# A GRU-fed expert layer: the stretch ahead of the recurrence in another order and in larger pieces

## The chip, the cores and the metric

One core of a Trainium2 chip runs the whole program. The metric is device microseconds (us) of one execution. Five engines take part: TensorE (PE), VectorE (DVE), ScalarE (ACT), GpSimd (POOL) and SyncE (SP); the last issues most of the transfers. Each engine runs its own list of instructions in order, and they meet through semaphores only.

## The reference

A GRU runs over 256 time steps for 8 sequences of width 512, and its states feed an expert layer with 8 experts (two per token) and a shared expert. What the change touches lies ahead of the first time step.

```python
def cell(h, x):                        # 256 times, one after the other
    gi = x @ W_ih + b_ih               # x: (8, 256, 512), W_ih: (512, 1536)
    gh = h @ W_hh + b_hh               # W_hh: (512, 1536)
    i_r, i_z, i_n = jnp.split(gi, 3, axis=-1)
    h_r, h_z, h_n = jnp.split(gh, 3, axis=-1)
    r = jax.nn.sigmoid(i_r + h_r)
    z = jax.nn.sigmoid(i_z + h_z)
    n = jnp.tanh(i_n + r * h_n)
    return (1.0 - z) * n + z * h
...
logits = h @ w_gate                    # softmax, the two best of 8 experts
gu = jnp.einsum('th,ehf->etf', h, w_gate_up); act = silu(g) * u
routed = combine of jnp.einsum('eti,eih->eth', act, w_down)
return x + routed + silu_and_mul(h @ w_sh_gate_up) @ w_sh_down
```

## The kernel before, in words

Every float32 matrix is kept as two float16 halves, a high and a low one, and a product of two matrices takes three float16 products (`PROD`). To split a matrix it must be scaled by a power of two, and that needs a bound of its largest magnitude first. So each matrix goes through the same steps: its transfer lands; it is scanned (VectorE takes a row maximum with `rowmax`, ScalarE a row sum of magnitudes with `accum_out`, each over a part of it); the bounds of several matrices are spread over all 128 partitions by two tiny TensorE products, `spread_cross` and `spread_back`, with VectorE's `spread_rows` and `spread_scale` between and behind them; `floors` makes scales of them and releases `scaled`; then `high` on ScalarE writes the high half of a piece and `low` on VectorE the low half.

There are three such rounds ahead of or early in the recurrence. Round 1 holds x's first block (`PX0`) and W_ih (`PIH`). Round 2 holds W_hh, the router's weights, h0 and x's block 1 (`PHH` and the three behind it). Round 3 holds the rest of x (`PX`).

A weight matrix of 512 x 1536 lies in 12 slots of 128 x 512. The raw float32 numbers lie `SHIFT = 2` slots behind the place of their halves, so a high half may be written only when the low half of two slots before has been read (the wait on `ih_lo` or `hh_lo` in `high_ih` and `high_hh`).

`gates(n, c)` on TensorE multiplies W_ih with a block of 32 time steps of x: n // 12 is the block, n % 12 the slice of 128 output columns, and c the quarter of the inner width. The 12 products of block 0 come ahead of the recurrence, with six PSUM banks; the first six fill them, and n = 6 and on wait until `gates_out` (ScalarE for even n, VectorE for odd n) has emptied the bank. Later blocks are spread over the time steps by `make_plan`, a list scheduler: for each piece of work it has an engine, a cost in us, what it comes after, an earliest step and a due step. From it come the orders of all engines within the loop over t.

A time step is `recur(t)` on TensorE (32 small products into psG), then `step(t)` on VectorE, which begins with two transposes out of psG and ends with the new state, and three tanh on ScalarE between. Behind `step(t)` every engine does its planned work of that step, and ScalarE then `keep(t)`. `place(t)` puts the input gates of step t beside psG's numbers; VectorE's second transpose waits for it.

Right ahead of step 0, VectorE's list ends with `x_low(1)`, the low half of x's block 1, and ScalarE's with `x_high(1)` and three sums of x's rest, `sum_x(3)` to `sum_x(5)`; `sum_x(0)` to `sum_x(2)` stand behind the sum over W_hh.

## Time and profile before

| what | value |
|---|---|
| three runs, median (lowest to highest) | 1200.42 us (1195.88 to 1204.8) |
| profiled execution, its own time | 1195.19 us |
| span of its trace | 1193.4 us |
| busy: PE, DVE, ACT, POOL | 87%, 71%, 48%, 17% |
| first transpose of step 0, of the last step | 51.33 us, 1033.57 us |

The span runs from the first to the last record of the trace; 1.8 us of the execution lie outside it. A share of busy time is a mean over the whole program: up to 51.33 us no time step has begun, up to about 1037 us the 256 steps run, and the rest is the tail of the expert layer.

### The profile page before, as it was taken

Reading aid. Unit: us, or ns where it says so; the run is one execution under the profiler, and the core shown is the slowest. Engines: PE = TensorE matmul, PEld = TensorE weight load, DVE = VectorE, ACT = ScalarE, POOL = GpSimd, SP = SyncE. Lnnn points to the kernel's source line nnn. Section 1 sums busy time; section 2 is a strip of 40 time slices with the busy share of each in tenths; the row PEclk is TensorE's granted clock in tenths of the full one; section 3 lists DMA queues with packets and bytes.
Section 4 is the critical chain, followed back from the end, with each engine's and each line's share of the span. In section 5 each row is a group of like instructions: output and inputs, shape, how many; then the busy total and the mean of one; then the engine's idle time right before and its main releaser. Section 6 shows DMA issues by size and latency. Waiting matters only on the chain.

```text
span 1193.4 us, 35909 instructions
## 1 busy us (share of the span) xinstructions
PE 1036.9 (87%) x13452; PEld 623.1 (52%) x13452; DVE 850.0 (71%) x4089; ACT 573.3 (48%) x1877; POOL 206.2 (17%) x213
## 2 busy tenths in 40 slices
PE   2789888889999898999899989998998898889894
PEld 2556555556665454555455545554555454555452
DVE  5898999868889888677867787678787778721111
ACT  4755555655555543445344434443444444435442
POOL 0200011020110212111211121112120112233332
PEclk9999999999999999999999999999999999999897
DMA  8943455381864753623451234234342144488694
GB/s 307 402 147 97 144 180 186 107 205 56 294 237 173 197 193 73 230 75 61 125 178 29 55 101 166 56 55 174 129 126 55 28 143 134 121 296 278 181 288 56
DMA packets 68829, 183.13 MB, mean 153 GB/s; under 512 B 7737, under 2 KB 40288, under 8 KB 61344
## 3 DMA queue, kind: packets, MB, share of 16 engines
q1 hardware_dynamic: 45632, 107.74, 25.5%
q0 software_dynamic: 23024, 73.11, 23.1%
q8 instruction: 106, 1.74, 0.6%
q14 instruction: 67, 0.55, 0.2%
HBM read 137.01 MB, written 52.87 MB: 159 GB/s over the span
## 4 chain that ended last, share of the span: by engine, by line
PE 51%; DVE 27%; ACT 10%; issue 7%; DMA 3%; POOL 0%; POOLq 0%; SPq 0%; ACTq 0%; DVEq 0%
PE psG L715 17%; PE psG L721 14%; PE psU L778 6%; DVE arena L1046 5%; DVE arena L1044 5%; ACT arena L1429 4%; ACT arena L1425 4%; PE psS L824 3%; DVE arena L1054 3%; DVE arena L1069 3%; DVE arena L1065 3%; DVE arena L1056 3%; PE psD L790 3%; DVE arena L1048 2%; PE psO L845 2%
## 5 line engine op out<-in xcount | busy, mean ns | idle before, releaser
L715 PE MATMUL psG<-arena 128*32 128x384 f16 x4096 | 213.8, 329 | 76.1 <-DVE arena L1069 68.2
L1425 ACT ACTIVATE arena<-arena 128x32 f32<-128x32 f32 x256 | 58.6, 229 | 336.7 <-DVE arena L1048 335.3
L721 PE MATMUL psG<-arena 128*32 128x384 f16 x4096 | 211.9, 327 | 3.7 <-issue 3.7
L778 PE MATMUL psU<-arena 128*128 128x256 f16 (+1 forms) x1920 | 203.7, 253 | 0.2 <-DVE arena L940 0.2
L1044 DVE STREAM_TRANSPOSE arena<-psG 128x128 f32<-128x128 f32 x256 | 81.1, 317 | 144.8 <-PE psG L721 138.2
L778 PEld LDWEIGHTS psU<-arena 128*128 128x128 f16 x1920 | 157.7, 99 | 49.1 <-issue 13.6
L715 PEld LDWEIGHTS psG<-arena 128*32 128x32 f16 x4096 | 86.2, 96 | 175.0 <-DVE arena L1069 141.9
L1625 POOL DMA_INDIRECT y<-arena x55 | 87.6, 1593 | 393.4 <-DVE arena L1046 312.2
L721 PEld LDWEIGHTS psG<-arena 128*32 128x32 f16 x4096 | 109.9, 97 | 60.9 <-issue 4.4
L1046 DVE STREAM_TRANSPOSE arena<-psG 128x256 f32<-128x256 f32 x256 | 104.1, 407 | 0.0
L790 PE MATMUL psD<-arena 128*128 128x512 f16 x384 | 97.6, 382 | 4.9 <-DVE arena L1264 4.9
L824 PE MATMUL psS<-arena 128*128 128x512 f16 x372 | 92.3, 380 | 1.7 <-ACT arena L1497 1.5
L1441 ACT ACTIVATE arena<-arena 128x64 f16<-128x64 f16 x256 | 63.9, 250 | 37.1 <-DVE arena L1074 36.1
L1429 ACT ACTIVATE arena<-arena 128x32 f32<-128x32 f32 x256 | 58.7, 229 | 39.4 <-DVE arena L1056 16.3
L940 DVE SCALAR_TENSOR_TENSOR arena<-arena 128x1024 f16<-128x1024 f32 (+1 forms) x68 | 73.4, 1091 | 2.7 <-ACT arena L1334 2.3
L1427 ACT ACTIVATE arena<-arena 128x32 f32<-128x32 f32 x256 | 58.7, 229 | 26.8
L1334 ACT ACTIVATE arena<-arena 128x1024 f16<-128x1024 f32 (+1 forms) x68 | 66.4, 986 | 8.3 <-DVE arena L940 4.2
L700 PE MATMUL psS<-arena 128*128 128x256 f16 x528 | 67.0, 273 | 1.0 <-issue 0.7
L700 PE MATMUL psO<-arena 128*128 128x256 f16 x528 | 67.4, 276 | 0.0
L1065 DVE TENSOR_TENSOR arena<-arena 128x32 f32<-128x32 f32 x256 | 49.2, 192 | 22.4 <-ACT arena L1429 0.7
L1051 DVE TENSOR_REDUCE arena<-arena 128x32 f32<-128x96 f32 x256 | 64.0, 250 | 0.0
L1050 DVE TENSOR_REDUCE arena<-arena 128x32 f32<-128x96 f32 x256 | 63.1, 246 | 0.0
(166 smaller groups left out, 1557.7 us busy)
## 6 DMA issues: line engine op xcount, KB each, us to landing
arena<-expert_weights SPq DMA_DIRECT2D x39, 1536.0 KB, 8.6
arena<-wgu POOLq DMA_DIRECT2D x32, 512.0 KB, 5.5
expert_weights<-arena POOLq DMA_DIRECT2D x9, 1536.0 KB, 6.8
gi_scratch<-arena SPq DMA_DIRECT2D x84, 128.0 KB, 2.0
arena<-gi_scratch SPq DMA_DIRECT2D x14, 768.0 KB, 5.6
arena<-wd POOLq DMA_DIRECT2D x16, 512.0 KB, 5.7
arena<-x SPq DMA_DIRECT2D x8, 512.0 KB, 4.0
hidden_rows<-arena SPq DMA_DIRECT2D x16, 256.0 KB
```

The lines of the kernel that those rows point to most:

```text
L700: r = e.matmul(ps, half(W_IH + fc // 4 * 4 + c, pw)[:, (fc % 4) * 128:(fc % 4) * 128 + 128], x_half(b, c // 2, px)[:, (c % 2) * 256:(c % 2 ...
L715: e.matmul(psG[32 * j:32 * j + 32, 0:384], prev[:, c, 2:6].rearrange("p q n -> p (q n)"), whv[c][1][:, :, :, 32 * j:32 * j + 32], start=(c ...
L721: r = e.matmul(psG[32 * j:32 * j + 32, 0:384], prev[:, c, 0:4].rearrange("p q n -> p (q n)"), whv[c][0][:, :, :, 32 * j:32 * j + 32], star ...
L778: r = e.matmul(psU[u % 2][:, 256 * gu:256 * gu + width], half(W_GS + ex * 4 + c, pw)[:, o:o + 128], hh[:, 1 - ph, c, first:first + width], ...
L790: r = e.matmul(ps[:, 0:512], AH[u % 3][:, pa, tc * 128:tc * 128 + 128], half(W_DS + n, pw), start=(n == 0 and j == 0), stop=(n == 7 and j ...
L824: r = e.matmul(up_bank(k)[:, 0:512], hT[k % 2][:, ph, c], ew_half(k, c, pw), start=(c == 0 and j == 0), stop=(c == KC - 1 and j == 2))
L1044: e.transpose(Tt[:, 0:4, 0:32], psG[:, 0:128].rearrange("p (f m) -> p f m", m=32)).then_inc(tr_r, 1)
L1046: e.transpose(Tt[:, 4:12, 0:32], psG[:, 128:384].rearrange("p (f m) -> p f m", m=32)).then_inc(tr_zn, 1)
L1065: e.tensor_tensor(zc, zc, qq, ALU.mult).then_inc(g_m, 1)
L1425: e.activation(Ur, Ur, ACT.Tanh, scale=reg_tr).then_inc(th_r, 1)
L1429: e.activation(qq, qq, ACT.Tanh, scale=reg_tn).then_inc(th_n, 1)
L1625: e.indirect_dma_start(y, by(index), out, None, compute_op=ALU.add).then_inc(added, 16)
```

## The change: what it does

- The transfers of W_ih and W_hh are cut: four of 768 KB for W_ih, and 768, 768, 768, 256 and 512 KB for W_hh, each with a semaphore of its own. x's block 1 has its own place (`x_src(1)`, slots 8 and 9 of ring 0) and is issued before the small loads and without a wait; before, it came behind them and waited until `x_low(0)` had been done. The raw weights lie four slots behind their halves (`WSHIFT = 4`), the last two slots of W_hh's raw numbers in ring 1.
- W_ih is scanned in quarters as they land; the last quarter is shared by VectorE and ScalarE (768 columns each).
- W_hh's bound is taken earlier: ScalarE sums slots 0 to 2 ahead of `x_high(0)`, and slots 3 to 5 and 10, 11 behind the first third of W_ih; VectorE takes slots 6 to 9 there. x's block 1 is bounded by ScalarE (`x1_sum`) instead of VectorE.
- Round 2's `spread_cross` stands behind gates n = 1 and `spread_back` behind n = 2; before, both stood behind n = 3.
- `high_ih`, `high_hh`, `low_ih` and `low_hh` take two slots (128x1024) at a time: 6 instructions for each matrix and engine where there were 12.
- Of block 0's `gates_out`, ScalarE takes 8 and VectorE 4 (before 6 and 6).
- `recur(0)` waits for W_hh's low halves by quarters of the inner width, not for all at once.
- `x_low(1)` moves behind step 0. The six `sum_x` move behind steps 0 to 3 (2, 2, 1, 1). Round 3 moves from steps 1 to 4 to steps 4 to 7. In the plan, gates of block 1 begin at step 1, `scan_load` and `d_sum` at step 3, x's block 2 at step 8. The plan has 363 steps as before; from step 42 on, every step holds the same work as before.

The instructions of TensorE from the first product of gates to the second time step, before (psU, psD, psS and psO are the banks of gates, psT that of the bounds, psG that of the recurrence):

```order
3 L700 MATMUL psU<-arena 128x256 x24
4 L700 MATMUL psD<-arena 128x256 x24
5 L676 MATMUL psT<-arena 4x128
6 L680 MATMUL psT<-arena 128x4
7 L700 MATMUL psS<-arena 128x256 x12
8 L700 MATMUL psO<-arena 128x256 x12
9 L700 MATMUL psU<-arena 128x256 x24
10 L700 MATMUL psD<-arena 128x256 x24
11 L700 MATMUL psS<-arena 128x256 x12
12 L700 MATMUL psO<-arena 128x256 x12
13 L715 MATMUL psG<-arena 32x384 x16
```

And the same stretch of TensorE in the changed kernel:

```order
3 L709 MATMUL psU<-arena 128x256 x24
4 L685 MATMUL psT<-arena 4x128
5 L709 MATMUL psD<-arena 128x256 x12
6 L689 MATMUL psT<-arena 128x4
7 L709 MATMUL psD<-arena 128x256 x12
8 L709 MATMUL psS<-arena 128x256 x12
9 L709 MATMUL psO<-arena 128x256 x12
10 L709 MATMUL psU<-arena 128x256 x24
11 L709 MATMUL psD<-arena 128x256 x24
12 L709 MATMUL psS<-arena 128x256 x12
13 L709 MATMUL psO<-arena 128x256 x12
14 L725 MATMUL psG<-arena 32x384 x16
```

The first bounding product of round 2 (psT, 4x128) moved ahead by 24 matmuls and the second by 12; the rest stands as it did.

ScalarE from the split of W_ih to step 0, before (128x2x512 is x, 128x512 a slot of a weight matrix; 128x1024 x3 are the sums over x's rest, 128x2x128 the emptying of a bank, 128x8x8 `place`):

```order
4 L1334 ACTIVATE arena<-arena 128x512 x8
5 L1391 ACTIVATE arena<-arena 128x4608
6 L1369 ACTIVATE arena<-arena 128x1024 x3
7 L1334 ACTIVATE arena<-arena 128x512 x4
8 L1360 ACTIVATE arena<-psU,arena 128x2x128
...
20 L1411 ACTIVATE arena<-arena 128x8x8
21 L1334 ACTIVATE arena<-arena 128x2x512
22 L1369 ACTIVATE arena<-arena 128x1024 x3
23 L1420 TENSOR_LOAD arena
24 L1421 TENSOR_LOAD arena
25 L1425 ACTIVATE arena<-arena 128x32
```

ScalarE in the changed kernel, from the sums of W_ih to the end of step 0:

```order
4 L1361 ACTIVATE arena<-arena 128x1536
5 L1348 ACTIVATE arena<-arena 128x2x512 x3
6 L1361 ACTIVATE arena<-arena 128x1536
7 L1361 ACTIVATE arena<-arena 128x1024
8 L1417 ACTIVATE arena<-arena 128x1024
9 L1348 ACTIVATE arena<-arena 128x2x512 x5
...
25 L1443 TENSOR_LOAD arena
26 L1444 TENSOR_LOAD arena
27 L1448 ACTIVATE arena<-arena 128x32
28 L1450 ACTIVATE arena<-arena 128x32
29 L1452 ACTIVATE arena<-arena 128x32
30 L1436 ACTIVATE arena<-arena 128x8x8
31 L1389 ACTIVATE arena<-arena 128x1024 x2
```

The sum over nine slots of W_hh became sums of three, three and two, and the sums over x's rest left the stretch ahead of the tanh of step 0 (L1425, now L1448); two of them stand behind it.

The diff, cut to its core:

```diff
+WSHIFT = 4
...
-            p.add("PE", ("gates", n, c), 0.37, before, due=due)
+            p.add("PE", ("gates", n, c), 0.37, before, step=1, due=due)
...
+        def ih_raw(k, n):
+            return raw(W_IH + WSHIFT + k, n)
+
+        def hh_raw(k, n):
+            return ring(1, 6 + k - 10, n) if k >= 10 else raw(W_HH + WSHIFT + k, n)
+
+        def x_src(b):
+            return ring(0, 8, 2) if b == 1 else view(xp_raw, 1024, F32)
...
-            for q in range(2):
-                piece(wih, raw(W_IH + SHIFT + 6 * q, 6), 6 * q, 6, ld_ih[q])
-            for q in range(2):
-                piece(whh, raw(W_HH + SHIFT + 6 * q, 6), 6 * q, 6, ld_hh[q])
+            for q in range(4):
+                piece(wih, ih_raw(3 * q, 3), 3 * q, 3, ld_ih[q])
+            for q, (k, n) in enumerate(((0, 3), (3, 3), (6, 3), (9, 1), (10, 2))):
+                piece(whh, hh_raw(k, n), k, n, ld_hh[q])
+            load(x_src(1), x[:, 1024:2048], ld_x1)
...
-            e.wait_ge(x_lo, 1)
-            load(view(xp_raw, 1024, F32), x[:, 1024:2048], ld_xp)
+            e.wait_ge(hh_sum, 3)
             piece(x, ring(0, 0, 6), 4, 6, ld_xrest[0])
-            e.wait_ge(hh_sum, 1)
             piece(x, ring(1, 0, 6), 10, 6, ld_xrest[1])
...
                 for c in range(KC):
+                    if t == 0:
+                        e.wait_ge(hh_lo, (2, 3, 5, 6)[c])
...
-            for n in range(4):
-                for c in range(KC):
-                    gates(n, c)
-            spread_cross(2, PHH, 4)
-            spread_back(2, 4)
-            for n in range(4, 12):
+            for n in range(12):
+                if n == 2:
+                    spread_cross(2, PHH, 4)
+                if n == 3:
+                    spread_back(2, 4)
                 for c in range(KC):
                     gates(n, c)
...
             def low_hh(k):
-                low(raw(W_HH + SHIFT + k, 1), half(W_HH + k, 0), half(W_HH + k, 1), col(SHH), hh_hi, k + 1, hh_lo)
+                at = CH * (W_HH + 2 * k)
+                low(pair(hh_raw(2 * k, 2)), halves(at, 0), halves(at, 1), col(SHH), hh_hi, k + 1, hh_lo)
...
             x_low(0)
-            for k in range(8):
+            for k in range(2):
                 low_ih(k)
+            for q in (2, 3):
+                e.wait_ge(ld_hh[q], 16)
+            link(rowmax(mx[:, 38:39], hh_raw(6, 4)))
             e.wait_ge(ld_small, 128)
...
+            e.wait_ge(hh_sum, 3)
+            e.wait_ge(x1_sum, 1)
+            rowmax(gcol[:, PHH:PHH + 1], mx[:, 36:40]).then_inc(spread_cols, 1)
+            low_ih(2)
             spread_rows(2, 4)
+            low_ih(3)
...
-            for k in range(12):
-                if k % 2:
-                    gates_out(k)
+            for k, ready in enumerate(((), (1, 4), (), (7,), (), (10,))):
+                for n in ready:
+                    gates_out(n)
                 low_hh(k)
...
-            x_low(1)
...
             e.wait_ge(ld_ih[1], 16)
+            sum_weights(ih_raw(3, 3), ring(1, 0, 3), 42, ih_sum)
+            e.wait_ge(ld_ih[3], 16)
+            sum_weights(ih_raw(9, 3)[:, 768:1536], ring(1, 3, 3)[:, 0:768], 45, ih_sum)
+            e.wait_ge(ld_hh[0], 16)
+            sum_weights(hh_raw(0, 3), ring(0, 0, 3), 36, hh_sum)
             e.wait_ge(scaled, 1)
             x_high(0)
-            for k in range(8):
+            for k in range(2):
                 high_ih(k)
+            e.wait_ge(ld_hh[1], 16)
+            sum_weights(hh_raw(3, 3), ring(0, 3, 3), 37, hh_sum)
+            e.wait_ge(ld_hh[4], 16)
+            sum_weights(hh_raw(10, 2), view(hb0 + 4096, 1024, F32), 39, hh_sum)
+            e.wait_ge(ld_x1, 16)
+            e.activation(view(hb0 + 8192, 1024, F32), x_src(1), ACT.Abs, accum_out=gcol[:, PX1:PX1 + 1]).then_inc(x1_sum, 1)
+            for k in range(2, 6):
                 high_ih(k)
...
-            for k in range(3, 6):
-                sum_x(k)
...
+                for k in ((0, 1), (2, 3), (4,), (5,))[t] if t < 4 else ():
+                    sum_x(k)
```

## Rows read from the trace of the kernel before

**Rows 1.** The page: shares of the span in the chain that ended last.

```profile
PE 51%; DVE 27%; ACT 10%; issue 7%; DMA 3%; POOL 0%; POOLq 0%; SPq 0%; ACTq 0%; DVEq 0%
```

**Rows 2.** Timeline of VectorE, first transpose of steps 0, 1, 8, 53, 255.

```profile
51.33 0.31 DVE L1044 STREAM_TRANSPOSE arena<-psG 128x128 f32<-128x128 f32 x1
...
55.95 0.32 DVE L1044 STREAM_TRANSPOSE arena<-psG 128x128 f32<-128x128 f32 x1 [1.26 <-PE psG L721]
...
83.23 0.32 DVE L1044 STREAM_TRANSPOSE arena<-psG 128x128 f32<-128x128 f32 x1
...
261.05 0.32 DVE L1044 STREAM_TRANSPOSE arena<-psG 128x128 f32<-128x128 f32 x1 [5.22 <-PE psG L721]
...
1033.57 0.32 DVE L1044 STREAM_TRANSPOSE arena<-psG 128x128 f32<-128x128 f32 x1 [1.01 <-PE psG L721]
```

**Rows 3.** Timeline of VectorE up to step 0 (start, length, instruction, idle before).

```profile
12.85 1.94 DVE L915 TENSOR_REDUCE arena<-arena 128x1 f32<-128x1536 f32 x2 [0.35 <-DMA arena<-wih]
...
18.41 2.61 DVE L940 SCALAR_TENSOR_TENSOR arena<-arena 128x1024 f16<-128x1024 f32 x3 [1.22 <-ACT arena L1334]
...
29.16 1.41 DVE L915 TENSOR_REDUCE arena<-arena 128x1 f32<-128x2 f32 x2 [1.43 <-ACT arena L1391]
...
34.70 1.41 DVE L940 SCALAR_TENSOR_TENSOR arena<-arena 128x512 f16<-128x512 f32 x2
...
49.15 0.15 DVE L936 SCALAR_TENSOR_TENSOR arena<-arena 128x1 f32<-128x1 f32 x1
...
50.13 1.28 DVE L940 SCALAR_TENSOR_TENSOR arena<-arena 128x1024 f16<-128x1024 f32 x1
```

**Rows 4.** Timeline of ScalarE up to the first tanh of step 0.

```profile
12.85 1.48 ACT L1383 ACTIVATE arena<-arena 128x1536 f32<-128x1536 f32 x1 [10.82 <-DMA arena<-wih]
...
24.94 4.03 ACT L1391 ACTIVATE arena<-arena 128x4608 f32<-128x4608 f32 x1
...
28.97 1.04 ACT L1369 ACTIVATE arena<-arena 128x1024 f32<-128x1024 f32 x1
...
48.83 1.13 ACT L1334 ACTIVATE arena<-arena 128x1024 f16<-128x1024 f32 x1
...
52.99 0.21 ACT L1425 ACTIVATE arena<-arena 128x32 f32<-128x32 f32 x1
```

**Rows 5.** Timeline of TensorE: gates, round 2's two products, the first recur.

```profile
22.68 5.10 PE L700 MATMUL psU<-arena 128*128 128x256 f16 x24 [6.29 <-DVE arena L940]
27.62 2.78 PE L700 MATMUL psD<-arena 128*128 128x256 f16 x24
30.63 0.38 PE L676 MATMUL psT<-arena 128*4 128x128 f32 x2 [0.23 <-DVE arena L915]
31.38 0.38 PE L680 MATMUL psT<-arena 4*128 4x4 f32 x2 [0.37 <-DVE arena L928]
...
49.28 0.84 PE L715 MATMUL psG<-arena 128*32 128x384 f16 x16 [2.08 <-DVE arena L940]
```

**Rows 6.** Windows of 1 us, TensorE: busy (instructions), granted clock, DMA share, GB/s.

```profile
24.00:25.00 1.00, 1.00 (x6) 1.00 1.04 442
...
39.00:40.00 1.00, 1.00 (x7) 0.50 0.84 356
```

**Rows 7.** Transfers issued from 2.5 to 3.2 us: KB each, us to landing.

```profile
arena<-wih SPq DMA_DIRECT2D x1, 1536.0 KB, 10.7
arena<-whh SPq DMA_DIRECT2D x1, 1536.0 KB, 13.9
```

**Rows 8.** Transfers issued from 20.0 to 20.3 us, the same columns.

```profile
arena<-x SPq DMA_DIRECT2D x1, 1536.0 KB, 7.0
arena<-x SPq DMA_DIRECT2D x1, 512.0 KB, 3.7
```

**Rows 9.** Timeline of SyncE's queue: issue of the last small load.

```profile
11.30 3.16 SPq L578 DMA_DIRECT2D arena<-bhh  x1
```

**Rows 10.** Transfers issued from 11 to 12 us: KB each, us to landing.

```profile
arena<-bhh SPq DMA_DIRECT2D x1, 6.0 KB, 10.5
```

128 lines of the change are left out of this document (62 added, 66 removed).

## The prediction

> **What bounds the kernel now.** I read the chain of waits first. It is half TensorE and a quarter VectorE [rows 1], so no engine alone is the bound: what sets the end is a serial chain. The list of VectorE's first transposes shows which. From step 53 to step 255 they are 772.52 us apart for 202 steps, 3.82 us each [rows 2], and what is planned beside the steps fits into them with little over. The changed plan holds the same work in every step from 42 on, so behind that step a saving neither grows nor shrinks: the whole tail comes as much earlier as step 42 does. The question is thus where step 0 begins (51.33 us), how long it takes (4.62 us, against 3.8) and what steps 1 to 41 add.
>
> Next I read the three engines ahead of step 0. The reader is to see that nobody is idle for long, but that the work comes in a row. VectorE has W_ih's bound at 14.79 us, two microseconds behind the landing [rows 3]; TensorE starts the gates at 22.68 us and comes to round 2 of the bounds at 30.63 us, which VectorE's columns released at 30.57 us [rows 3, 5], and these waited for ScalarE's 4.03 us sum over W_hh, begun only at 24.94 us [rows 4], although W_hh's first half had landed at 2.62 + 13.9 = 16.5 us [rows 7]. From 34.70 to 49.15 us VectorE takes lows and banks without a pause worth the name [rows 3]: this stretch of 14.45 us is bound by VectorE. Then come small instructions and `x_low(1)`, and step 0. In step 0 VectorE had its numbers early, but ScalarE's first tanh began at 52.99 us, behind three sums over x's rest [rows 4].
>
> **The change part by part**, in the trace's own time.
>
> *W_ih's bound.* Its last transfer lands at 12.8 us as before, if pieces stream. Behind it stood a row maximum over 1536 columns and a tiny one, 1.94 us together [rows 3]; the last quarter is now shared, 768 columns each: half of 1.77, and 0.17, is 1.05 us on VectorE. On ScalarE the 768 columns are 0.75 to 0.95 us by half of 1.48 [rows 4] and something fixed: level. **-0.9 us**; the columns stand at 13.9.
>
> *To the gates.* From the columns to `x_low(0)` it took 14.79 to 18.41, 3.6 us, and this stays, if the new sum over slots 0 to 2, ahead of `x_high(0)`, is through by then. It begins when the first W_hh piece lands, halfway between 12.8 and 16.5, at 14.7, and takes 1.6: 16.3, against the release of `scaled` at about 16.4. It just fits; if it lands later, each 0.1 us costs 0.1. Then x and two W_ih pieces of 1024 columns: 1.28 and twice 1.19 (x3 of mixed size took 2.61, and pieces overlap by 0.09) is 3.7, where five pieces took 4.2. The gates start at 17.5 + 3.8 = 21.3. **-1.4 us** in all.
>
> *Round 2.* ScalarE ends the second W_ih piece at 19.7 and then has sums over 1536, 1024 and 1024 columns (1.48, 1.04, 1.04 and 0.1 between [rows 4]): 23.4. VectorE's 2048 columns are 2.3 us from 21.3 on. So the columns stand at 23.8 instead of 30.57. But TensorE is then within gates 0 and 1, ahead of round 2 in its list. Their 24 matmuls took 5.10 us, the next 24 took 2.78 [rows 5], and at 24 us six matmuls passed in 1 us, about as at 39 us, where the granted clock is recorded as 0.50, that is 1.2 GHz [rows 6]; the 1.00 recorded at 24 us I do not believe. Again TensorE comes out of about 5 idle microseconds (before, 6.29 [rows 5]), so I take the slow 5.1: `spread_cross` at 26.3, **-4.3 us**. If the clock rises sooner, 3.9 instead of 5.1 gives 25.1; if all of gates 2 is slow too, 1.2 later. `spread_back` stood 0.75 behind `spread_cross`; now twelve matmuls stand between, 1.4 at the fast rate, and VectorE's `low_ih(3)`, 1.28, runs under them: 28.0 against 31.38, **-3.4 us**. From there to VectorE's first free moment it took 34.70 - 31.38 = 3.3 and does so again: 31.3.
>
> *Lows and banks.* Before, 16 slots and 6 banks in 14.45 us [rows 3]. A pair of slots was 1.41 alone, 1.6 with ScalarE's turn; a piece of 1024 is 1.28 [rows 3], and overlapping 1.19. Now 8 pieces and 4 banks (0.45 each, what is left of 14.45 when 16 slots at 0.66 and 1.2 of waits are taken off, over 6): 9.5 + 1.8 = 11.3, and 0.1 of waiting. ScalarE's turn of 1.13 a piece [rows 4] plus 8 banks at 0.45 stays under it. VectorE is through at 42.7 against 49.15, **-6.4 us** in all. TensorE keeps up: gates 7 waits for VectorE's bank 1 until about 35.3, then five products at 1.35 end at 42.1. The last quarter of W_hh's low halves is what `recur(0)` waits for: its products end at 43.7, when VectorE is through with its small instructions (1.0 us, 49.15 to 50.13). `x_low(1)`, 1.2 us ahead of the transposes, is gone. Step 0 starts at 43.8 instead of 51.33: **-7.5 us**.
>
> *Step 0.* No sums stand ahead of the tanh, so it should take the ordinary 3.81: **-0.8 us**, and -8.3 us at step 1. The cover of what moved: `x_low(1)`, 1.28, lies in VectorE's idle end of step 0 (matmuls of `recur(1)`), and TensorE needs it just behind; two sums, 2.2 us, lie in what ScalarE has free in a step, which I put at 2.7 us: 3.81 less four short instructions of some 0.21 [rows 4] and the waits between them.
>
> *Steps 1 to 41.* Before, steps 1 to 7 took 27.28 us [rows 2], 0.6 over seven plain ones, for round 3; the same VectorE work is there, only later. New is that step 1 holds two sums, a bank and `keep` (2.9 us in the 2.7) and step 3 two sums and a bank (2.9), and that TensorE has 21 gate matmuls in steps 1 and 3: **+0.3 us**. The transfers they trigger (`scan_load` at x_sum 3 and 6, steps 1 and 3) have until step 9.
>
> Sum: -7.5 - 0.8 + 0.3 = **-8.0 us**. The profiled execution of 1195.19 would become 1187.2. It lay 5.2 us below the median of the runs; I subtract from the median: 1200.42 - 8.0 = **1192.4 us**.
>
> Bounds: step 0 at 43.3 (fast clock early) to 45.0 (gates 2 slow, a late landing), and +0 to +2 in steps 1 to 41: a gain of 4.5 to 8.5 us, so 1191.9 to 1195.9, and beside it the spread of medians; three runs lay 9 us apart.
>
> **The rivals.**
>
> *Pieces pay for themselves.* W_ih landed at 12.8 and W_hh's first half at 16.5, 3.7 us for 1.5 MB, while a load of 512 KB that found the queue empty took 3.7 from issue to landing and the 1536 KB behind it landed 3.7 later [rows 7, 8]. For: nothing shows pieces under 1.5 MB one behind the other. Against: that 512 KB did not delay its follower. If each additional piece cost 1.9 (3.7 less the 1.8 of its bytes at the streaming rate is the fixed part), W_ih's bound would come 3.8 us later and the end with it: 1196.2. The Trainium skill, "DMA: Bandwidth & Descriptors", section "Measured (HBM→SBUF, 128 partitions, SWDGE, issued from GpSimd)", asks for transfers of at least 1 MiB to reach 75% of peak, and speaks against the cut; at three quarters of the rate it too would put W_ih some 3 us later. Pieces of a full queue are not what rows 8 show delayed, so 7 in 100.
>
> *The small loads come last (slower).* They now stand behind x's block 1 and seven further pieces, and round 2 needs all eight (`ld_small`). The last was held 3.16 us at its issue and landed at 11.30 + 10.5 = 21.8 [rows 9, 10]. My estimate is 22.8: 1.2 later for the 512 KB ahead of them. They decide from about 25 us on, and each microsecond beyond costs one. If the hold is paid by each of the eight, because the queue is full of pieces by then, 8 x 3.16 from about 9.9 is 35, landing at about 37: step 0 at 55.6, 4.3 later than before, and the end at 1200.42 + 4.3 - 0.8 + 0.3 = 1204.2. [...] 6 in 100.
>
> *Given back in the first steps.* ScalarE's sums overrun, gates come late behind `x_low(1)`, and stores of gates compete with W_gu and W_d, whose loads go out at the same pace as before but meet earlier steps. Each slip of a tanh lengthens a step. Seven steps at +0.4 give back 3 us: 1195.4. 15 in 100.
>
> *The single stall.* Step 53 begins 261.05, 5.22 us after VectorE fell idle, waiting for TensorE [rows 2], which waited for nothing shown, in the middle of a recur. It costs some 4.7 us. The changed list has the same matmuls up to there, so I leave it where it is. The Trainium skill, "Runtime: NRT & Kernel Launch", section "Instruction fetch mechanics", says that instructions come in blocks by a queue of their own and that this is mostly hidden; if this was a fetch under the loads of that moment, it can vanish or come twice. Gone: 1187.7, 6 in 100; a second one: 1197.1, 6 in 100.
>
> **How the numbers follow.** Forecast 60 in 100, its own range 1188.5 to 1197.5. The likeliest is 1192.4; I give 1192.5. The range for 8 in 10 takes in the spread of the runs and the rivals but the slower one: 1186.5 to 1199.5. A measurement of this kernel can tell about 1% (12 us) from no change. Faster by over 1% needs 1188.4 or less: the vanished stall and the low side of the forecast, 0.17. Slower by over 1% needs more than the worst rival, 0.03. Within 1%: 0.80.
>
> **What would show it.** Right: gates at about 21.3 us, `spread_cross` of round 2 released by TensorE itself at 26, not by VectorE; step 0's first transpose at 43.3 to 45; step 1 3.8 us later; step 8 about 8 us earlier than before; steps from 42 on unchanged. Wrong: a first piece of W_ih or a small load that VectorE waits for beyond 25 us; a slow clock in gates 7 to 11 (1.2 us for each twelve matmuls); steps 1 to 20 above 3.9 us; a new stall of TensorE under the scan loads.

## The result, and the profile after

The changed kernel takes 1191.28 us (median) against 1203.3 us for the kernel before on the same chip, a ratio of 0.9905 (95% interval 0.9881 to 0.9929), -11.4 us. Two later repeats on two chips gave 0.9934 (0.9909 to 0.9959) and 0.9925 (0.9902 to 0.9947), -8.0 and -9.0 us. The mean of the three ratios is 0.9921, or -9.5 us. The forecast was -8.0 us and 1192.5. That 1191.28 lies so close to 1192.5 is in part luck: the forecast started from 1200.42, the median of three runs of the kernel before, which over eight runs is 1203.3. As a gain, -11.4 is more than the 4.5 to 8.5 us that the prediction gave for it; the repeats of -8.0 and -9.0 lie in it and just beyond it.

The timeline of VectorE in the kernel after, in the same columns as [rows 2] and [rows 3]: the last scans of W_ih, the pieces of W_hh, then the first transposes of steps 0, 1, 8, 42, 50, 53, 54 and 255.

```profile
11.14 3.08 DVE L924 TENSOR_REDUCE arena<-arena 128x1 f32<-128x1536 f32 x3 [2.00 <-DMA arena<-wih]
17.83 3.68 DVE L949 SCALAR_TENSOR_TENSOR arena<-arena 128x1024 f16<-128x1024 f32 x3 [1.22 <-ACT arena L1348]
21.43 2.66 DVE L924 TENSOR_REDUCE arena<-arena 128x1 f32<-128x2048 f32 x4
...
30.87 3.67 DVE L949 SCALAR_TENSOR_TENSOR arena<-arena 128x1024 f16<-128x1024 f32 x3
...
41.25 1.27 DVE L949 SCALAR_TENSOR_TENSOR arena<-arena 128x1024 f16<-128x1024 f32 x1
...
43.63 0.32 DVE L1056 STREAM_TRANSPOSE arena<-psG 128x128 f32<-128x128 f32 x1
...
47.43 0.32 DVE L1056 STREAM_TRANSPOSE arena<-psG 128x128 f32<-128x128 f32 x1
...
74.70 0.31 DVE L1056 STREAM_TRANSPOSE arena<-psG 128x128 f32<-128x128 f32 x1
...
204.88 0.32 DVE L1056 STREAM_TRANSPOSE arena<-psG 128x128 f32<-128x128 f32 x1
...
237.75 0.32 DVE L1056 STREAM_TRANSPOSE arena<-psG 128x128 f32<-128x128 f32 x1 [2.23 <-remote]
...
251.12 0.32 DVE L1056 STREAM_TRANSPOSE arena<-psG 128x128 f32<-128x128 f32 x1 [2.45 <-PE psG L731]
254.92 0.32 DVE L1056 STREAM_TRANSPOSE arena<-psG 128x128 f32<-128x128 f32 x1
...
1027.75 0.32 DVE L1056 STREAM_TRANSPOSE arena<-psG 128x128 f32<-128x128 f32 x1 [1.01 <-PE psG L731]
```

The columns of W_ih stand at 14.22 us, and VectorE is through with the pieces at 42.52 (before 49.15 [rows 3]). Step 0 starts at 43.63 us against 51.33 [rows 2], step 1 at 47.43 against 55.95, step 8 at 74.70 against 83.23. From step 53 (251.12) to step 255 it is 776.6 us here, 772.5 before: no part of the gain comes from there.

TensorE in the kernel after, its first products up to recur(0), answers to [rows 5]:

```profile
21.57 4.33 PE L709 MATMUL psU<-arena 128*128 128x256 f16 x24 [5.75 <-DVE arena L949]
25.83 0.38 PE L685 MATMUL psT<-arena 128*4 128x128 f32 x2
26.14 1.48 PE L709 MATMUL psD<-arena 128*128 128x256 f16 x12
27.55 0.38 PE L689 MATMUL psT<-arena 4*128 4x4 f32 x2
...
35.14 1.47 PE L709 MATMUL psU<-arena 128*128 128x256 f16 x12 [1.86 <-DVE arena L967]
...
41.78 1.15 PE L725 MATMUL psG<-arena 128*32 128x384 f16 x16
42.75 0.82 PE L731 MATMUL psG<-arena 128*32 128x384 f16 x16
```

The row at 25.83 has no bracket: round 2's product waits for nobody, only for the 24 slow matmuls ahead of it. VectorE's columns had been there since 21.43 + 2.66 = 24.09 us.

ScalarE in the kernel after, against [rows 4]: the sum over the first W_hh piece in the gap ahead of `x_high(0)`, and the first tanh, which VectorE alone releases now.

```profile
14.89 1.48 ACT L1361 ACTIVATE arena<-arena 128x1536 f32<-128x1536 f32 x1 [0.94 <-DMA arena<-whh]
...
16.65 3.23 ACT L1348 ACTIVATE arena<-arena 128x1024 f16<-128x1024 f32 x3 [0.18 <-DVE arena L933]
...
44.45 0.23 ACT L1448 ACTIVATE arena<-arena 128x32 f32<-128x32 f32 x1 [0.67 <-DVE arena L1060]
```

### The profile page after: what moved, and what is told of

Read it like the earlier page. It is cut to its first block, busy times and chain, and to the rows that moved or that the text cites. A ratio compares the mean times of both kernels' runs of the same rounds, so it can differ in the third digit from the quotient of the medians.

```text
span 1187.0 us, 35881 instructions
## 1 busy us (share of the span) xinstructions
PE 1033.3 (87%) x13452; PEld 621.2 (52%) x13452; DVE 846.4 (71%) x4075; ACT 574.1 (48%) x1875; POOL 206.3 (17%) x213
## 3 DMA queue, kind: packets, MB, share of 16 engines
q8 instruction: 106, 1.74, 0.6%
## 4 chain that ended last, share of the span: by engine, by line
PE 51%; DVE 26%; ACT 8%; issue 8%; DMA 4%; POOL 1%; another core or an unknown queue 0%; POOLq 0%; SPq 0%; DVEq 0%; ACTq 0%
PE psG L725 17%; PE psG L731 14%; PE psU L788 5%; DVE arena L1058 5%; DVE arena L1056 5%; ACT arena L1448 3%; ACT arena L1452 3%; DVE arena L1066 3%; DVE arena L1081 3%; DVE arena L1068 3%; PE psD L800 3%; PE psS L834 3%; DVE arena L1077 3%; DVE arena L1060 2%; PE psO L855 2%
## 5 line engine op out<-in xcount | busy, mean ns | idle before, releaser
L725 PE MATMUL psG<-arena 128*32 128x384 f16 x4096 | 214.0, 329 | 77.8 <-DVE arena L1081 68.4
L1448 ACT ACTIVATE arena<-arena 128x32 f32<-128x32 f32 x256 | 58.7, 229 | 333.3 <-DVE arena L1060 333.3
L731 PE MATMUL psG<-arena 128*32 128x384 f16 x4096 | 211.8, 326 | 1.6 <-issue 1.6
L788 PE MATMUL psU<-arena 128*128 128x256 f16 (+1 forms) x1920 | 203.5, 253 | 0.2 <-DVE arena L949 0.2
L788 PEld LDWEIGHTS psU<-arena 128*128 128x128 f16 x1920 | 157.5, 98 | 48.7 <-issue 12.9
L725 PEld LDWEIGHTS psG<-arena 128*32 128x32 f16 x4096 | 86.3, 96 | 176.9 <-DVE arena L1081 140.5
L731 PEld LDWEIGHTS psG<-arena 128*32 128x32 f16 x4096 | 110.0, 97 | 59.1 <-issue 2.5
L949 DVE SCALAR_TENSOR_TENSOR arena<-arena 128x1024 f16<-128x1024 f32 x56 | 71.2, 1278 | 1.7 <-ACT arena L1348 1.6
L709 PE MATMUL psS<-arena 128*128 128x256 f16 x528 | 67.4, 273 | 0.5 <-ACT arena L1384 0.3
L709 PE MATMUL psO<-arena 128*128 128x256 f16 x528 | 66.1, 273 | 0.4 <-ACT arena L1384 0.4
L1348 ACT ACTIVATE arena<-arena 128x1024 f16<-128x1024 f32 x56 | 63.3, 1136 | 4.4 <-DVE arena L949 3.2
## 6 DMA issues: line engine op xcount, KB each, us to landing
arena<-gi_scratch SPq DMA_DIRECT2D x14, 768.0 KB, 5.5
```

Of the source, the lines that this page charges most:

```text
L709: r = e.matmul(ps, half(W_IH + fc // 4 * 4 + c, pw)[:, (fc % 4) * 128:(fc % 4) * 128 + 128], x_half(b, c // 2, px)[:, (c % 2) * 256:(c % 2 ...
L725: e.matmul(psG[32 * j:32 * j + 32, 0:384], prev[:, c, 2:6].rearrange("p q n -> p (q n)"), whv[c][1][:, :, :, 32 * j:32 * j + 32], start=(c ...
L731: r = e.matmul(psG[32 * j:32 * j + 32, 0:384], prev[:, c, 0:4].rearrange("p q n -> p (q n)"), whv[c][0][:, :, :, 32 * j:32 * j + 32], star ...
L788: r = e.matmul(psU[u % 2][:, 256 * gu:256 * gu + width], half(W_GS + ex * 4 + c, pw)[:, o:o + 128], hh[:, 1 - ph, c, first:first + width], ...
L1448: e.activation(Ur, Ur, ACT.Tanh, scale=reg_tr).then_inc(th_r, 1)
```

## The experiments

There were twelve runs, in three groups of four; the runs of a group share a chip and the executions of the kernel before, whose medians were 1206.02, 1201.16 and 1195.77 us. Differences in microseconds are a ratio times that median; the plain difference of two medians is up to 1.6 us off from it. "Changed kernel" is the kernel after. The changed kernel was run in the first and third groups, and there no 95% interval of a variant lies clear of its own; so the medians alone tell little and the traces carry the argument.

### Both kernels again

*The kernel before, unchanged.* 

> The kernel before, unchanged, for a second trace of it. Theory A (the gain is the stretch up to step 1, the rest is scatter): the first transpose again at 51.3 us and step 1 at 55.9 us, within 0.3; the ratio to the runs of before 1.000 within 0.003; what differs from the first trace (span 1193.4 us) is how long single steps between 8 and 255 are held up. Theory B (the stall of TensorE at step 53 is a property of the kernel before): the step before 53 is again above 6 us. Rival C (the stall is chance): a plain 3.8 us there and stalls elsewhere.

Measured: 0.9993 (0.9972 to 1.0014), so the comparison tells some 0.2% from nothing. Step 0 came at 52.14 us, 0.8 later than expected, and step 1 at 56.04, as expected. The step before 53 again took over 6 us (7.65), so theory B holds and rival C falls.

*The changed kernel, unchanged.* 

> The changed kernel, unchanged, for a second trace. Theory A: step 0 at 43.6 us, step 1 at 47.4 us, step 8 at 74.7 us, each within 0.3, and a ratio to before of 0.993 (8.0 us, the sum of the prediction), if the scatter of single steps is the same in both. Rival D (the change also lessens the stalls behind step 42): a ratio of 0.990 again, and fewer or shorter held-up steps than in the traces of before.

Measured: 0.9934 (0.9909 to 0.9959), -8.0 us, as expected. The trace missed: step 0 came at 44.00 us, step 1 at 49.08 and step 8 at 76.40, 0.4, 1.7 and 1.7 later than expected. *And once more, in the third group.* 

> The changed kernel once more, so that the other kernels of this call have it on their own chip: between 8 and 11.4 us under the kernel before, the two differences seen so far. Step 0 at 43.6 to 44.0 us in its trace; a hold of 1.7 to 2.2 us at step 49 and of 1.9 to 5 us at steps 52 and 53.

Measured: 0.9925 (0.9902 to 0.9947), -9.0 us. Its step 0 came at 44.68 us, 0.7 later than expected; the hold at step 49 did not come, and that at steps 52 and 53 took 8.60 and 5.67 us, 6.6 us in excess. Five traces of the two kernels give the start of steps in a table:

```
trace          step 0   step 1   step 42   step 48   step 54
before          51.33    55.95    214.16    237.01    265.58
before again    52.14    56.04    214.25    237.11    264.24
after           43.63    47.43    204.88    227.74    254.92
after again     44.00    49.08    206.58    229.44    259.75
after, third    44.68    49.62    207.41    230.26    260.07
```

At step 42 the changed kernel is ahead by 9.3, 7.6 and 6.8 us, 7.9 in the mean. From 42 to 48 all five take 22.85 or 22.86 us. From 48 to 54 they take 28.57, 27.13, 27.18, 30.31 and 29.81, where the six steps alone would take 22.9. So what the change is known to do is done at step 42. From step 54 to step 255 the two traces of the kernel before take 768.0 and 773.6 us, the three of the changed kernel 772.8, 775.7 and 768.4; five traces can't tell whether anything of the gain is given back there.

### Larger pieces

```diff
-                at = CH * (W_IH + 2 * k)
-                low(pair(ih_raw(2 * k, 2)), halves(at, 0), halves(at, 1), col(SIH), ih_hi, k + 1, ih_lo)
+                for s in (2 * k, 2 * k + 1):
+                    low(ih_raw(s, 1), half(W_IH + s, 0), half(W_IH + s, 1), col(SIH), ih_hi, s + 1, ih_lo)
```

and so for W_hh, for ScalarE's high halves and for the waits on them.

> The changed kernel with the low halves of both weights computed again in 16 pieces of 512 columns instead of 8 of 1024; scans, landings, round 2 and the order of the sums stay as changed. If the larger pieces are worth what the sum of the prediction took (14.45 us of pieces before against 11.4), step 0 starts 2 to 3 us later than the changed kernel's 43.6 to 44.0 us and the median is 2 to 3 us higher. If the pieces pay for themselves (VectorE was already waiting for ScalarE's high halves and not for its own work), step 0 moves by less than 0.5 us and so does the median.

Measured: 0.9947 (0.993 to 0.9963), -6.4 us. The changed kernel itself has no run in this group; its three runs elsewhere had -8.0 to -11.4, and the next kernel, in this group, -10.0. VectorE's timeline of the same stretch, and one row of TensorE:

```profile
31.28 4.06 DVE L949 SCALAR_TENSOR_TENSOR arena<-arena 128x512 f16<-128x512 f32 x6
...
41.53 1.42 DVE L949 SCALAR_TENSOR_TENSOR arena<-arena 128x512 f16<-128x512 f32 x2 [0.85 <-ACT arena L1348]
...
43.40 1.41 DVE L949 SCALAR_TENSOR_TENSOR arena<-arena 128x512 f16<-128x512 f32 x2
```

```profile
35.94 2.72 PE L709 MATMUL psU<-arena 128*128 128x256 f16 x12 [2.25 <-DVE arena L967]
```

Six pieces of 512 take 4.06 us where three of 1024 take 3.67. From the first piece to the last VectorE needs 13.53 us, against 11.65 in the changed kernel, and step 0 starts at 45.91, 1.2 to 2.3 us later than in its three traces. Of the 1.9 us between the two, 0.85 is a wait for ScalarE's high half: TensorE's twelve matmuls took 2.72 us here, against 1.47, so ScalarE had to wait 2.00 us for the bank psD ahead of that half. TensorE had stood idle for 2.25 us ahead of them, against 1.86; whether the smaller pieces brought this about or chance did, one trace can't tell, and the profiled execution, 1205.61 us, lay 10 us above the median of its kernel. What is left, 1.0 us, is VectorE's own pieces, as the prediction had it (16 slots at 0.66 against 8 pieces at 1.19). So the theory holds for about half of the 1.9 us; step 0 comes 2 us later than in the two faster traces with both halves of it.

### Round 2 of the bounds, later and sooner

```diff
-                if n == 2:
-                    spread_cross(2, PHH, 4)
-                if n == 3:
-                    spread_back(2, 4)
+                if n == 4:
+                    spread_cross(2, PHH, 4)
+                    spread_back(2, 4)
```

> The changed kernel with both products of round 2 behind gates 3 again. Theory A (TensorE's list sets round 2): spread_cross 2.6 us later (28.5 instead of 25.8), and since low_ih(3) then stands between VectorE's maximum and its scales, 2.2 to 2.5 us later at the first transpose (46.0). Rival (the lows bind VectorE anyway, so round 2 may come later): under 1 us.

Measured: 0.9942 (0.9921 to 0.9963), -7.0 us, 1.0 us slower than the changed kernel beside it; the intervals overlap. The trace is clearer: TensorE's round 2 and the wait that comes of it,

```profile
21.60 4.93 PE L709 MATMUL psU<-arena 128*128 128x256 f16 x24 [5.75 <-DVE arena L948]
...
29.08 0.38 PE L685 MATMUL psT<-arena 128*4 128x128 f32 x2
...
38.12 1.47 PE L709 MATMUL psU<-arena 128*128 128x256 f16 x12 [2.80 <-DVE arena L966]
```

and step 0 at 46.61 us, 2.6 later than the changed kernel of that group. Theory A holds in the trace, with both times 0.6 us later than worked out.

The other way, `spread_cross` ahead of gates 1 (n == 1) and `spread_back` ahead of gates 2, with VectorE's `spread_rows` ahead of `low_ih(2)` and `low_ih(3)` behind `floors`:

> The changed kernel with round 2 of the spread sent by TensorE before it starts on the gates of the second quarter, not after, and with VectorE's part of it ahead of the low half of the third quarter. Theory: TensorE reaches round 2 at 25.8 us with nothing to wait for, since its own slow matmuls stand in front of it; put ahead of them it goes at about 24.1, the scale is known 1.7 us sooner, and about 1 us of that reaches step 0, so the median is 1 us lower. Rival: the low halves on VectorE set the end alone, and whatever round 2 gains is given back in a wait for the next low half: step 0 within 0.3 us, the median unchanged.

Measured: 0.9917 (0.9898 to 0.9937), -10.0 us. TensorE:

```profile
21.75 2.74 PE L709 MATMUL psU<-arena 128*128 128x256 f16 x12 [5.75 <-DVE arena L949]
24.43 0.42 PE L685 MATMUL psT<-arena 128*4 128x128 f32 x2
```

Round 2 goes at 24.43 us, 1.4 sooner than in the kernel after, but step 0 starts at 43.34, 0.3 sooner: 18.91 us behind `spread_cross(2)`, where it is 17.80 in the kernel after. So 1.1 us is given back on VectorE, which now has `low_ih(3)` and the setting up one behind the other, instead of a piece of 1.26 us under TensorE's products. Against the kernel after the rival holds; against the other two traces of the changed kernel (44.00 and 44.68) step 0 is 0.7 and 1.3 sooner, as the theory had it. The medians can't tell 1 us.

### W_ih's scans by pairs of quarters

```diff
-            e.wait_ge(ld_ih[0], 16)
+            for q in range(2):
+                e.wait_ge(ld_ih[q], 16)
             link(rowmax(mx[:, 41:42], ih_raw(0, 3)))
-            e.wait_ge(ld_ih[2], 16)
+            for q in (2, 3):
+                e.wait_ge(ld_ih[q], 16)
```

and the same two waits ahead of ScalarE's sums.

> The changed kernel with W_ih's scans waiting for its quarters in pairs: scans 0 and 1 start when quarter 1 has landed, the rest when quarter 3 has; each scan stays the same size and on the same engine. Theory: what the quarters buy is the scan of quarter 2 beside the landing of quarter 3. Without it VectorE scans 1.75 and 0.95 us after the last landing at about 13.0, so the columns are ready at 15.8 and not 14.2, and with nothing to catch up on behind them step 0 and the median are 1.2 to 1.6 us later. Rival: later on VectorE waits 1.2 us for ScalarE's high half and ScalarE waits for W_hh, so half of it is caught up: 0.5 us.

Measured: 0.995 (0.9919 to 0.9982), -6.0 us, 3.0 us slower than the changed kernel beside it; the intervals overlap. TensorE:

```profile
23.24 4.45 PE L709 MATMUL psU<-arena 128*128 128x256 f16 x24 [5.76 <-DVE arena L949]
27.62 0.38 PE L685 MATMUL psT<-arena 128*4 128x128 f32 x2
```

The gates start 1.44 us later than in the changed kernel's trace of this group (21.80), step 0 only 0.74 later (45.42 against 44.68). Not by VectorE's catching up, as the rival had it: the same 24 matmuls took 4.45 us here and 5.15 there, so round 2 went 0.75 later (27.62 against 26.87), and step 0 followed it to the hundredth. In the three traces of the changed kernel and in this one step 0 comes 17.80, 17.80, 17.81 and 17.80 us behind `spread_cross(2)`. That product, held by TensorE's slow start, sets the stretch.

### The sums of x back ahead of step 0

```diff
             place(0)
             x_high(1)
+            for k in range(3):
+                sum_x(k)
```

with one more in each of steps 0 to 2, as before, and `x_low(1)` back ahead of step 0.

> The changed kernel with one part undone: x_low(1) and three of the sums over x's rest stand ahead of step 0 again. Theory A: VectorE has 1.2 us more ahead of the first transpose (44.9 instead of 43.6), and ScalarE's first tanh comes at 46.9 behind x_high(1) (42.7 to 43.8) and three sums (3.2), 1.1 later than the transposes ask: step 1 at 49.8 instead of 47.4, the whole 2.4 us slower than the changed kernel. Rival (the steps behind absorb it, since there they have fewer sums): less than 1 us slower.

Measured: 0.9955 (0.9933 to 0.9977), -5.4 us, 2.5 us slower than the changed kernel beside it (by the medians 1.0); the intervals overlap. ScalarE's third sum and its first tanh in this kernel:

```profile
45.77 1.04 ACT L1388 ACTIVATE arena<-arena 128x1024 f32<-128x1024 f32 x1
46.81 0.21 ACT L1449 ACTIVATE arena<-arena 128x32 f32<-128x32 f32 x1
```

The tanh comes 1.8 us behind the transposes of 45.02 and step 0 takes 6.02 us. The changed kernel has its tanh 0.82 us behind them, so the sums cost 1.0 us of step 0. Step 0 starts 1.0 later than in the changed kernel's trace of this group (`x_low(1)`), step 1 2.0, step 8 2.4, step 42 2.3. The price came out as expected, 2.4 us, in the trace and in the ratio. Step 1 itself came at 51.04 us, not 49.8, because `recur(1)` is slow here as well:

```profile
48.24 1.47 PE L725 MATMUL psG<-arena 128*32 128x384 f16 x16 [4.65 <-DVE arena L1082]
```

### The slow matmuls, and the holds at steps 49 and 52

Two things differ from trace to trace of one kernel. The first is TensorE's rate. In the second trace of the changed kernel `recur(1)` is slow. Its TensorE:

```profile
46.27 1.47 PE L725 MATMUL psG<-arena 128*32 128x384 f16 x16 [2.32 <-DVE arena L1081]
47.53 1.50 PE L731 MATMUL psG<-arena 128*32 128x384 f16 x16
```

and its window from 44 to 48 us (busy time and instructions of TensorE, of its weight loads, VectorE, ScalarE and GpSimd, then the granted clock, DMA share and GB/s):

```profile
44.00:48.00 4.00, 1.73 (x24) 0.92 (x28) 3.55 (x14) 3.07 (x10) 0.00 (x0) 0.75 0.52 217
```

The same stretch of the kernel after, at full clock:

```profile
44.00:48.00 4.00, 2.02 (x37) 1.27 (x38) 3.74 (x15) 3.06 (x9) 0.00 (x0) 1.00 0.55 229
```

Step 0 takes 5.08 us in the one and 3.80 in the other. The fast one is the exception. In all twelve traces of the changed kernel and its variants TensorE stands idle for 2.32 us or more ahead of `recur(1)`, and in ten of them it or the matmuls right behind it are slow: steps 0 and 1 together take 7.76 us in the kernel after and in one other, and 8.93 to 9.25 in nine more, 1.2 to 1.5 us longer (`sums_back`, with the sums on top, 10.45). Neither trace of the kernel before has this, for between `recur(0)` and `recur(1)` stood gates of block 1:

```profile
51.52 1.47 PE L700 MATMUL psS<-arena 128*128 128x256 f16 x12 [0.75 <-issue]
52.83 0.82 PE L700 MATMUL psO<-arena 128*128 128x256 f16 x6
```

The change moved them to step 1, since they need `x_low(1)`. What ScalarE's sums covered is something else and smaller: in the second trace of the kernel before `recur(0)` was slow, behind 3.19 idle microseconds, and step 0 came 0.8 us later, yet step 1 at 56.04 against 55.95, as the sums ended last either way. The sums do not cover a slow `recur(1)`, as their return shows: it took 1.47 us there too. No run keeps gates in step 0 of the changed kernel, so what that would give, 1.2 to 1.5 us by these traces less what the gates cost there, is an estimate.

The second is a hold of TensorE in `recur(53)`. The kernel before, TensorE:

```profile
255.53 0.33 PE L721 MATMUL psG<-arena 128*32 128x384 f16 x3
259.55 1.46 PE L721 MATMUL psG<-arena 128*32 128x384 f16 x13 [3.69 <-issue]
```

The kernel after:

```profile
248.35 0.33 PE L731 MATMUL psG<-arena 128*32 128x384 f16 x3
250.25 0.82 PE L731 MATMUL psG<-arena 128*32 128x384 f16 x13 [1.56 <-issue]
```

All twelve traces without added matmuls break that group of 16 at the same place, three and thirteen, for 0.90 to 4.06 us. In the five microseconds before TensorE went on there is one packet of the instruction queue q8, in each of the fourteen traces. The DMA view of such a window (packets, MB, share of 16 engines) in the kernel after, from 246.0 us:

```profile
q8 instruction: 1, 0.02, 38.4%
```

in the second run of it, from 250.0 us:

```profile
q8 instruction: 1, 0.02, 25.9%
```

and in the next kernel, from 248.0 us:

```profile
q8 instruction: 1, 0.02, 14.7%
```

Share times 16 engines times the window's 0.5 us is how long the packet took: 3.1, 2.1 and 1.2 us. The page of the kernel after has 106 of them at 0.6% of 16 engines' span, 1.1 us each, for 26904 matmuls and weight loads of TensorE, 254 a packet; the kernels with 40 more matmuls have 107. So q8 is very likely TensorE's. In windows of 0.1 us the packets start at 246.1, 250.3 and 248.2 us, so they ended at about 249.2, 252.4 and 249.4, and TensorE went on 1.0 to 1.3 us behind that. This speaks for a hold that ends when the packet is in. But in the third of them the packet had ended ahead of the hold (249.74 us), so its transfer alone does not fill the hold. Two kernels test this. The first moves the DRAM-to-DRAM copies that GpSimd issues at 235 us (y<-xt, hidden_rows<-hpad, with an expert's load right behind) to other steps, by the planner's numbers alone:

```diff
-        p.add("POOL", ("hid_init", b), ..., step=8 + 11 * b, due=8 + 11 * b)
-        p.add("POOL", ("y_init", b), ..., step=20 + 10 * b, due=20 + 10 * b)
+        hs = (8, 13, 25, 32, 41, 63, 74, 85)[b]
+        ys = (14, 25, 31, 40, 60, 70, 80, 90)[b]
+        p.add("POOL", ("hid_init", b), ..., step=hs, due=hs)
+        p.add("POOL", ("y_init", b), ..., step=ys, due=ys)
```

> The changed kernel with only the steps changed at which two kinds of DRAM-to-DRAM copies are issued (hidden_rows and y preset from x or padding), so that none is queued at 235 to 245 us, around steps 49 to 53. Theory: the holds at step 49 (about 6.0 us where its neighbours take 3.8) and step 52 (5.8 to 8.2 us) are instruction fetches that stand behind full DMA engines, so both go and the median is 3 to 4 us lower. Rival: they belong to the place in the code and not to what is queued on the DMA engines; they stay at their steps with their lengths, and the median is unchanged. Second rival: they move with the copies to other steps, and nothing is gained.

Measured: 0.9901 (0.9886 to 0.9915), -11.9 us. The two copies of 235 us are gone from there; one of y<-xt, at 246.37 us in the kernel after, is still issued at 247.42. The hold stays where it was, behind the third matmul, but it is the shortest of all, 0.90 us:

```profile
249.41 0.33 PE L733 MATMUL psG<-arena 128*32 128x384 f16 x3
250.64 0.82 PE L733 MATMUL psG<-arena 128*32 128x384 f16 x13 [0.90 <-issue]
```

Steps 49 and 52 are 5.15 and 5.09 us. So the holds did not go, against the theory. They are shorter than in the traces with the copies in place (5.55 to 6.20 us for step 49 where it is held, 5.75 us or more for step 52), against the rival; how much of that is chance one trace can't tell. With round 2 sooner as well:

> The last two edits together, as the version that would be the best one if both theories hold: 4 to 5 us under the changed kernel. If only the copies matter 3 to 4, if only round 2 does 1, and if neither the same median as the changed kernel within 0.1%.

Measured: 0.9927 (0.9915 to 0.994), -8.8 us, with steps 49 and 52 at 5.25 and 5.30 us and a hold of 1.12. It does not beat either edit alone, so the ratios do not show that either edit gains anything.

The second kernel adds 20 matmuls, in the place where TensorE is idle ahead of the gates:

```diff
             spread_back(1, 2)
+            for _ in range(20):
+                e.matmul(psG[:, 0:128], idf, idf, start=True, stop=True)
```

> The changed kernel with 20 more matmuls (identity times identity in float32, 128x128, into the recurrence's bank, whose content is overwritten) in TensorE's idle 5.75 us ahead of the first gates. First question, TensorE's slow start: if the 24 matmuls of gates 0 and 1, 4.33 us in the changed kernel against 1.47 for 12 later on, are slow because the engine had stood idle, they take about 3.0 us now, round 2 goes at 24.3 and not 25.8, and step 0 is up to 1 us sooner; if not, nothing moves. Second question, the holds at steps 49 and 52: if they come with the place in TensorE's stream of instructions (every trace has the hold of step 52 behind the third of the last 16 matmuls of recur(53)), the hold comes 20 to 40 matmuls earlier in the program; if it belongs to the transfers alone, it stays in the same place in time and moves by no such number.

Measured: 0.9943 (0.9915 to 0.9971), -6.8 us. TensorE at its start,

```profile
15.73 6.35 PE L868 MATMUL psG<-arena 128*128 128x128 f32 x40
21.91 2.78 PE L709 MATMUL psU<-arena 128*128 128x256 f16 x24
24.63 0.38 PE L685 MATMUL psT<-arena 128*4 128x128 f32 x2
```

and around the hold:

```profile
244.72 2.08 PE L788 MATMUL psU<-arena 128*128 128x256 f16 x9 [2.37 <-issue]
...
249.27 0.83 PE L731 MATMUL psG<-arena 128*32 128x384 f16 x16
```

Both questions have an answer. The 24 matmuls of gates 0 and 1 take 2.78 us, the full rate, instead of 4.33 to 5.15; round 2 goes at 24.63 us and step 0 starts at 42.78, the earliest of all traces. And the hold has moved: it stands now ahead of the 9 matmuls of L788, the 12 of L709, the 16 of L725 and the first 3 of L731, 40 that used to come before it. The 20 added float32 products are 40 matmuls in the row above. The hold is tied to a place in TensorE's list of instructions, and exactly. The packet does not explain its length: in a window from 240.0 us it took 11.9% of 16 times 0.5 us, 1.0 us. It started at 240.2 us, so it was over at 241.2, 1.1 us before the hold of 2.37 us began (242.35) and 3.5 before it ended. That step 0 is sooner is not seen in the ratio. The profiled execution also has a step 140 of 8.16 us, where TensorE waits 2.98 us for a transfer of expert_rows and then goes on slowly; in no other trace does that step take over 4.67 us.

The added matmuls are not free: they ended at 22.08 us, where the gates of the kernel after start at 21.57. Last, both together:

> The kernel with the copies moved away from steps 48 to 53, and the 20 matmuls of the last one: the version meant to be best. The moved copies shortened the holds at steps 49 and 52 from 4.0 us or more in sum to 2.6, so it is 1.4 us or more under the changed kernel of this call, and up to 1 us more if the priming works. Rival: the holds of this size are within what executions differ by, and the medians are the same within 0.1%.

Measured: 0.9899 (0.9864 to 0.9934), -12.1 us (by the medians -10.5), the lowest ratio of all, beside the changed kernel's 0.9925 on this chip. The intervals overlap. Its step 0 came at 43.48 us, for the added matmuls took 7.32 us here and the gates began at 22.96. Its hold is as long as that of the kernel without the moved copies (2.40 and 2.37 us), so with the instruction stream shifted the copies made no difference. A version that surely beats the changed kernel has not been found.

## Why the prediction was right, and where it was not

**W_ih's bound, gates.** Columns predicted at 13.9, measured 14.22 us (the quarter landed at 13.0, not 12.8); gates at 21.3, measured 21.57. The first W_hh piece landed at 14.9 and its sum ended at 16.4, just ahead of `x_high(0)`, as worked out. Four pieces of 768 KB, one behind the other, cost next to nothing beyond their bytes: all of W_ih is there 0.2 us later than in two pieces. The rival falls. Its price was also too low by its own rows: the 512 KB of [rows 8] are 1.2 us at the streaming rate, not 1.8, which would make the fixed part 2.5 us a piece. The rule that the prediction took from the Trainium skill, "DMA: Bandwidth & Descriptors", section "Measured (HBM→SBUF, 128 partitions, SWDGE, issued from GpSimd)", at least 1 MiB for 75% of peak, would have put W_ih some 3 us later by the prediction's estimate; the measured landing at 13.0 us shows no such loss for pieces queued behind each other.

**The small loads.** The last was issued and landed as these rows of the kernel after show, SyncE's queue first (start, length of the issue),

```profile
16.98 1.04 SPq L588 DMA_DIRECT2D arena<-bhh  x1
```

and the transfers issued from 16.9 to 17.1 us (KB each, us to landing), against [rows 9, 10]:

```profile
arena<-bhh SPq DMA_DIRECT2D x1, 6.0 KB, 6.5
```

That is 23.5 us, where 22.8 was estimated and 25 was the point from which it decides. VectorE did not wait for it: the row at 21.43 has no gap. On the way two issues together took 3.2 us and one 3.6, so the rival's mechanism was there twice and not eight times; by the prediction's 25 us, 1.5 us more would have made it the bound.

**Round 2.** Predicted at 26.3 us and released by TensorE itself; measured 25.83 and no wait. The prediction chose 5.1 us for the slow matmuls, with 3.9 as the other case; the three traces of the changed kernel have 4.33, 4.69 and 5.15, and those of its variants lie in between. The step rested on not believing the clock recorded there; the added matmuls, behind which the same 24 take 2.78 us, bear it out.

**Lows and banks.** VectorE free at 31.3, measured 30.87; gates 7 waits to 35.3, measured 35.14; through at 42.7, measured 42.52; recur(0) ends at 43.7, measured 43.57; step 0 at 43.8, measured 43.63, 44.00 and 44.68. The stretch of 14.45 us came down to 11.65 where 11.4 was worked out. Of the 2.8 us, 1.0 is VectorE's larger pieces, by the experiment; 0.9 is the two banks by the prediction's price of 0.45, which no run tests; the rest, 0.9, is waits between the pieces, for which the sum had 1.1.

**Step 0.** Predicted 3.81 us. It was 3.80 in one trace and 5.08 and 4.94 in the others, where `recur(1)` ran at the lower clock (0.50 from 46 to 48 us in the second), behind TensorE's 2.3 idle microseconds. The -0.8 us was right about the sums (1.0 us of step 0 in the experiment). What it left out is that the same change took the gates of block 1 out of TensorE's gap in this step; in the mean of the traces step 0 became 0.3 us longer and not 0.8 shorter.

**Steps 1 to 41.** Predicted +0.3. Step 1 to step 42 took 158.21 us before, twice, and 157.45, 157.50 and 157.79 after: -0.6 in the mean. The sums and gates in steps 1 and 3, which the rival feared, lengthened step 1 by 0.15 to 0.5 us and step 3 by nothing. The gain is between steps 8 and 42 (130.93 against 130.18), where the kernel before has lengthened steps at 11, 12, 25 and 32 and the changed one at 10, 12 and 33. The prediction held the plan of these steps equal in cost without reading them one by one. This term had the wrong sign and was off by 0.9 us. By its own terms the bounds were a little off too: step 0 at 43.3 to 45.0 and 0 to 2 us in the later steps make a gain of 5.1 to 8.8 us, not 4.5 to 8.5.

**The single stall.** It was left where it is, and it is there in every trace, at the same matmul. That much was right for the reason given (the same matmuls stand ahead of it), but as a term it is not a constant: the steps from 48 to 54 vary by 3.2 us over five traces of the two kernels. The Trainium skill, "Runtime: NRT & Kernel Launch", section "Instruction fetch mechanics", says that instructions are fetched in blocks by a queue of the engine's own and that crossing a block is mostly hidden; the shift by exactly 40 fits the blocks, and 0.90 to 4.06 us of TensorE's time was not hidden here. That the fetch is the cause is not shown, since in three traces the packet found was over before TensorE stopped.

**The sum.** At step 42 the three traces are ahead by 7.9 us in the mean, the sum was 8.0. This closeness is luck in part: step 0 came out 1.1 us worse than its term and steps 1 to 41 0.9 us better, and the two cancel. The first comparison's -11.4 is more than this; the repeats came to -8.0 and -9.0, so some 1.5 us between trace and median remain, inside what the medians can tell.

What stays open: what makes TensorE stop at that place, and for how long (the moved copies went with the two shortest holds, 0.90 and 1.12 us, and made no difference with the added matmuls: 2.40 against 2.37 us); and why VectorE is held some 2 us at step 49 (2.23 and 1.80 us in the kernel after and its second run, put down to "remote"). That step takes over 5 us in seven of the twelve traces of the changed kernel and its variants, in none of the two of the kernel before, and in none of the four traces of the third group.

## What to carry to other kernels

Look for the product that an in-order engine reaches late although its input is there: here a row without a bracket at 25.83 us set the whole stretch, and step 0 followed it at 17.80 us from trace to trace. When you move work to a later step, ask whose gap it filled; without the gates of block 1 TensorE stood idle for 2.3 us in step 0, and in ten of twelve traces what came next ran slowly. And when a hold stands at the same instruction in every trace, add instructions ahead of it: if it moves by just their number, it belongs to a place in the list of instructions and not to the work around it.

## What the runs showed of the hardware

The granted clock is recorded as 1.00 (2.4 GHz) from 20 to 28 us, while 24 matmuls take 4.33 us that take 2.78 us when TensorE was busy just before. The rate after an idle stretch differs between runs of one kernel: 4.33, 4.69 and 5.15 us for the same 24 matmuls after the same 5.75 us of idleness. After 2.3 idle microseconds ahead of `recur(1)` the matmuls ran at the lower rate in two traces of three.

TensorE stopped for 0.90 to 4.06 us at one place of its list in all fourteen traces, and 40 matmuls added ahead moved that place by 40. One 16 KB packet of q8 (1.74 MB over 106) stood in the five microseconds before it went on, and took 0.9 to 3.7 us where the mean is 1.1. After seven of the fourteen holds the matmuls ran slowly for a while: 2.08 us for nine that take 1.16 (at 245.25 us in the kernel after), 1.46 us for thirteen that take 0.82; the granted clock from 259.5 to 262.5 us in the kernel before is 0.51. There the cost is greater than the hold.

The DMA engines can be full with little: the kernel after moved 77 GB/s at a share of 0.96 from 234 to 240 us, 892 packets of some 0.5 KB in 0.46 MB. It is not the DRAM-to-DRAM copies issued there that fill them: with these moved away it is 73 GB/s at 0.88.
